# Values times output weights in three 16-bit products, with the step's instructions in a new order, in a decoder layer on one core

## The chip, the cores and the metric

The kernel runs on one core of one Trainium2 chip. The time is device microseconds for one execution, the median of three. Five engines work side by side and meet only at semaphores: TensorE (PE in the profile), VectorE (DVE), ScalarE (ACT), GpSimd (POOL) and SyncE (SP), which issues transfers. Each engine takes its own instructions in program order, so an instruction that waits holds up everything behind it on its engine.

## What is computed

One decoder layer on x of shape 8 x 128 x 256: a gated linear attention with a state per head, a cross attention over 256 positions, and a mixture of experts with a shared expert. Each is added to x after a layer norm. The change touches mostly the first one:

```python
x = x + _L0_attn_ref(_layernorm(x), ...)
x = x + _L0_xattn_ref(_layernorm(x), ctx, mask, mask, ...)
x = x + _L0_ffn_ref(_layernorm(x), ...)

# _L0_attn_ref: 16 heads, 128 key channels, 256 value channels, 128 positions, 8 batches
q = _causal_conv_silu(x @ Wq, qcw, qcb)      # a convolution with 4 taps, then silu
k = _causal_conv_silu(x @ Wk, kcw, kcb)
v = _causal_conv_silu(x @ Wv, vcw, vcb)
q = _l2norm(q); k = _l2norm(k)
alpha = sigmoid(x @ Wa); beta = sigmoid(x @ Wb)
def step(state, inp):
    qt, kt, vt, at, bt = inp
    state = state * at
    err = vt - einsum('bhkv,bhk->bhv', state, kt)
    state = state + bt * einsum('bhk,bhv->bhkv', kt, err)
    ot = einsum('bhkv,bhk->bhv', state, qt)
    return state, ot
out = outs.reshape(b, t, 32 * 128) @ Wo
```

## The kernel before, in words

**The recurrence as matrices.** The scan over 128 positions is not run as a scan. For a head and a batch the kernel forms the 128 x 128 lower part of keys times keys and of keys times queries with its decays (`lm`), inverts the unit triangular matrix by doubling (blocks of 2, 4, ... 128, the "levels"), and so has for each head a 128 x 128 matrix `pt` by which the values are multiplied. The output weights are folded in first: `z` is values times that head's rows of Wo (256 x 256), and the output is `pt` times z.

**Steps and slots.** A step is one head and one group of four batches: 16 heads x 2 groups = 32 steps. Work is software pipelined by hand. In slot k each engine runs a fixed list of calls that belong to up to five steps: `a` is step k+2 (projections, bias, taps of the convolution), `b0` is k+1 (norms, decays, first products), `b` is k (first levels of the inverse, z), `c` is k-1 (last levels, result), `d` is k-2 (output product). Slots -3 to 3 are written out, 4 to 27 run in a hardware loop with four slots in a pass, 28 to 33 are written out again. The order in which an engine's calls stand in `slot(k)` is the order in which they run.

**One slot by engine.** TensorE: `proj_(n)` (L1316), n = 0 to 3 for key, query and the two halves of the values, each six 16-bit products of 512 columns (x and weights split in high and low parts). `z(n)` (L1345), two halves of four 32-bit products of 256 columns. `outp` (L1515), `grams` (L1391) and `grams_later` (L1401) in 32 bits; the levels' products t1 (L1423) and pair (L1430, L1433); `residual` (L1481 to L1483), `y0` (L1493, L1494), `y1` (L1504), `norms` (L1359, L1360), `turn` (L1367), `exponents` (L1376, L1381), `b_first` (L1411). VectorE: twelve taps (L1030), level corrections (L998, L1010, L1013), the two halves of `lm` (`lmul` L1042, `lmul_later` L1053), the two output sums (L1060, L1067), `floor` (L1074) and `terms` (L1084, L1086). ScalarE: four `bias` (L728), the two `zcopy` (L721), the exponentials (L738), `v_silu` (L790), `k_silu` (L768), two squares (L775, L782), copies of t1 (L703 to L714), the logarithm (L754), two table loads. GpSimd: five masked copies `cut` (L501), the 16-bit split of `lm` (`lm_hi` L509 as an addition of zero, `lm_lo` L519), `sq_low_` (L487), four small parts (L527 to L533), and in every other slot the split of the next head's weights (L462, L464, L468).

**PSUM ring.** Banks 0 and 1 (`ubank`) go round z(0) or z(1), zcopy, a projection, its bias and three taps, the next projection, its bias and three taps, and back to z. So `z(0)` waits until the taps of projection 2 are done and `z(1)` until those of projection 3 are.

**Cross attention and experts.** The scores run as 64 units of two heads each. For a unit TensorE makes the scores for the row maximum (`top_scores`, L1638, 32 rows), VectorE reduces them (L1168), TensorE makes the scores again turned (`energies`, L1659, nine units behind), ScalarE takes the exponential (L849), and `values` (L1673, 128 rows by 32 columns) sums. In the experts, for each of 11 tiles of a group: `gate_up` (L1763), `spread_comb` (L1770, 16 rows) and `down` (L1786).

## Time and profile before

| | |
|---|---|
| median of 3 runs | 884.89 us (880.3 to 886.42) |
| the profiled execution | 882.86 us |
| its span | 881.1 us |
| its mean granted clock | 0.979 |
| PE / DVE / ACT / POOL busy | 92% / 80% / 72% / 57% |

The span is the part that the trace covers. The page gives each engine's busy time; other views list the work of a stretch by engine, the chain that ended last, and every instruction with its wait. Back-to-back records of one engine overlap by some 0.05 to 0.1 us, so the distance between two starts is what an instruction costs in a full queue, and its record is longer. A 32-bit product stands in the trace as two records.

### The profile page before, as it was taken

The page shows a single profiled execution, that of the slowest core. Times are in us where ns is not written, and L with a number is a line of the kernel's source. Part 1 is how long each engine was busy: PE and PEld are TensorE (multiplying, and loading weights), DVE is VectorE, ACT ScalarE, POOL GpSimd, SP SyncE. Part 2 cuts the span into 40 slices and gives each one's busy share as a digit, 9 for nine tenths or more (in the row PEclk, how much of TensorE's full clock was granted, in tenths as well). Part 3 has the DMA queues.
Part 4 walks back from the last instruction along what each step waited for, and adds up shares of the span by engine and source line. Part 5 has one row for each costly group of instructions (what it writes and reads, how often), then busy time and mean ns, then how long its engine had stood idle before and what let it go on. Part 6 is the DMA issues. An engine that isn't in the chain of part 4 may idle for free.

```text
span 881.1 us, 21906 instructions
## 1 busy us (share of the span) xinstructions
PE 811.9 (92%) x7458; PEld 526.2 (60%) x7458; DVE 707.2 (80%) x1221; ACT 630.2 (72%) x1052; POOL 501.6 (57%) x633
## 2 busy tenths in 40 slices
PE   3789999999999999999999999999889999989997
PEld 1356766767766777666677667776665333333353
DVE  7588888888888888888888888888566888874747
ACT  3588888888888888888888888888342377765522
POOL 7556959668585775868668596655612223331300
PEclk9799999999999999999999999999999999977999
DMA  5313011010110101001010110000000060000000
GB/s 140 99 27 85 2 38 38 2 37 0 36 35 0 36 0 36 11 25 36 0 36 0 36 36 0 12 2 2 1 2 24 9 108 24 21 21 18 8 24 25
DMA packets 35650, 23.97 MB, mean 27 GB/s; under 512 B 6260, under 2 KB 34644, under 8 KB 35469
## 3 DMA queue, kind: packets, MB, share of 16 engines
q1 hardware_dynamic: 32845, 18.98, 7.7%
q0 software_dynamic: 2752, 4.29, 2.4%
q8 instruction: 32, 0.52, 0.2%
q14 instruction: 21, 0.17, 0.1%
HBM read 22.64 MB, written 1.08 MB: 27 GB/s over the span
## 4 chain that ended last, share of the span: by engine, by line
PE 68%; DVE 14%; issue 9%; ACT 4%; POOL 3%; DMA 1%; SPq 1%; DVEq 1%; ACTq 0%; POOLq 0%
PE psum L1316 13%; PE psum L1345 12%; PE psum L1515 6%; DVE y L1030 6%; PE psum L1673 4%; PE psum L1401 3%; PE psum L1391 3%; DVE ux L1010 3%; PE psum L1423 2%; PE psum L1623 2%; PE psum L1659 2%; PE psum L1430 2%; PE psum L1638 2%; PE psum L1433 2%; PE psum L1763 1%
## 5 line engine op out<-in xcount | busy, mean ns | idle before, releaser
L1030 DVE SCALAR_TENSOR_TENSOR y<-psum,cwh,y 128x508 f32<-128x508 f32 (+2 forms) x384 | 281.6, 740 | 21.6 <-ACT y L728 15.5
L487 POOL TENSOR_TENSOR sql<-sq,sqh 128x1024 f16<-128x1024 f32 x32 | 68.4, 2138 | 135.7 <-ACT sq L775 135.7
L1345 PE MATMUL psum<-wo,vt 128*128 128x256 f32 x512 | 126.0, 389 | 1.2 <-DVE y L1030 1.0
L728 ACT ACTIVATE y<-psum,cwh 128x512 f32<-128x512 f32 x128 | 99.3, 776 | 29.5 <-PE psum L1316 28.7
L501 POOL TENSOR_TENSOR ct<-lm,levels 128x256 f16<-128x256 f32 x160 | 111.0, 711 | 6.8 <-DVE lm L1053 6.8
L1345 PEld LDWEIGHTS psum<-wo,vt 128*128 128x128 f32 x512 | 92.3, 190 | 11.9 <-DVE y L1030 2.0
L1168 DVE TENSOR_REDUCE mx<-psum 128x4 f32<-128x1024 f32 x64 | 77.6, 1220 | 12.7 <-PE psum L1638 12.4
L849 ACT ACTIVATE et<-psum 128x1024 f32<-128x1024 f32 x64 | 65.4, 1023 | 28.9 <-PE psum L1659 27.9
L1010 DVE TENSOR_TENSOR ux<-ux,psum 128x512 f16<-128x512 f16 x64 | 44.0, 687 | 51.9 <-PE psum L1433 50.8
L1316 PE MATMUL psum<-xth,whi 128*128 128x512 f16 x256 | 78.5, 389 | 6.6 <-POOL wlo L468 2.3
L1316 PE MATMUL psum<-xtl,whi 128*128 128x512 f16 x256 | 78.3, 388 | 0.0
L1316 PE MATMUL psum<-xth,wlo 128*128 128x512 f16 x256 | 78.0, 387 | 0.0
L519 POOL TENSOR_TENSOR lml<-lm,lmh 128x1024 f16<-128x1024 f32 x32 | 68.3, 2134 | 0.0
L998 DVE TENSOR_TENSOR ux<-ux,psum 128x512 f16<-128x512 f16 x96 | 65.1, 678 | 1.8 <-PE psum L1433 1.8
L1430 PEld LDWEIGHTS psum<-t1z,ux 128*128 128x128 f16 x768 | 45.6, 98 | 34.0 <-ACT t1z L714 10.0
L509 POOL TENSOR_TENSOR lmh<-lm,zero 128x1024 f16<-128x1024 f32 x32 | 60.5, 1891 | 0.1
L1515 PE MATMUL psum<-zz,pt 128*128 128x256 f32 x256 | 60.5, 379 | 0.0
L1430 PE MATMUL psum<-t1z,ux 128*128 128x64 f16 x768 | 54.0, 193 | 3.9 <-ACT t1z L714 2.0
L1515 PEld LDWEIGHTS psum<-zz,pt 128*128 128x128 f32 x256 | 48.5, 190 | 6.5
L790 ACT ACTIVATE vt<-y 128x1024 f32<-128x1024 f32 x32 | 33.8, 1057 | 23.9 <-issue 16.8
L738 ACT ACTIVATE decay<-psum,rc 128x256 f32<-128x256 f32 x128 | 50.1, 478 | 0.6 <-PE psum L1381 0.5
L1673 PE MATMUL psum<-et,vz 128*32 128x256 f32 x512 | 45.3, 429 | 0.5 <-ACT avs L856 0.3
(220 smaller groups left out, 1957.7 us busy)
## 6 DMA issues: line engine op xcount, KB each, us to landing
wraw<-in_L_attn_Wv SPq DMA_DIRECT2D x32, 128.0 KB, 2.7
wo<-in_L_attn_Wo SPq DMA_DIRECT2D x16, 256.0 KB, 2.8
wraw<-in_L_attn_Wk SPq DMA_DIRECT2D x16, 128.0 KB, 2.5
wraw<-in_L_attn_Wq SPq DMA_DIRECT2D x16, 128.0 KB, 2.9
moved<-avs SPq DMA_DIRECT2D x128, 16.0 KB, 1.8
x<-in_x SPq DMA_DIRECT2D x8, 128.0 KB, 4.0
maskrow<-in_mask_row POOLq DMA_DIRECT2D x1, 1024.0 KB, 5.4
xt<-in_ctx SPq DMA_DIRECT2D x1, 1024.0 KB, 6.4
```

What stands on the lines that cost most here:

```text
L487: g.tensor_tensor(lo, f, hi, ALU.subtract).then_inc(sq_split, 1)
L501: g.tensor_tensor(dst, src, pick.unsqueeze(1).to_broadcast([P, NB, T // (2 * m), m]), ALU.mult).then_inc(masked[l], 1)
L519: g.tensor_tensor(lo, f, hi, ALU.subtract).then_inc(lm_low, 1)
L728: s.activation(y[:, n], ubank[n % 2].rearrange("p (j t) -> p j t", j=NB), ACT.Identity, scale=cwh[:, (a.c // 2) % 2, n, TAPS - 1:TAPS], bi ...
L1010: v.tensor_tensor(changed(r, m), changed(r, m), cx.rearrange("p (a q u) -> p a q u", a=2, u=m), ALU.subtract).then_inc(uxc_sb, 1)
L1030: v.scalar_tensor_tensor(out=y[:, n, :, sh:], in0=u[:, :, 0:T - sh], scalar=cwh[:, (a.c // 2) % 2, n, TAPS - 1 - sh:TAPS - sh], in1=y[:, n ...
L1168: v.tensor_reduce(mx[:, h % 2, g2, 2 * rp:2 * rp + 2].rearrange("p r a -> p (r a)"), pair_of("max", n).rearrange("p r (a s) -> p (r a) s", ...
L1316: mm = t.matmul(ubank[n % 2], w_[:, hr, n, ch, :], x_[:, ch, cols], start=(m == 0), stop=(m == len(ops) - 1))
L1345: mm = t.matmul(ubank[n][:, j * H:(j + 1) * H], vt[:, r, vc, (2 * n + j) * T:(2 * n + j + 1) * T], wo[:, hr, vc, :], start=(vc == 0), stop ...
L1430: mm = t.matmul(half(dst[:, 256 + j * 64:256 + (j + 1) * 64], m), turned(st.c % 2, 0, j), first_half(t1z[:, level - 1, j * T:(j + 1) * T], ...
L1515: mm = t.matmul((ctk, cx)[hf][:, jj * H:(jj + 1) * H], pt[:, j], zz[:, d.c % 2, j], start=True, stop=True)
L1673: mm = t.matmul(avb[ps, gq // 2 * H:(gq // 2 + 1) * H], vz[:, b % 2, st, r, gq], et[:, gn % 4, r, st], start=(gq == 0 and st == 0), stop=( ...
```

## The change

**z in 16 bits.** The values get a high and a low part (`vth`, `vtl`), so do the output weights (`woh`, `wol`), and `z(n)` is now, for each of its four 32-bit products, three 16-bit ones of 256 columns. ScalarE applies silu a second time to write `vth` (`v_high`), and GpSimd subtracts (`v_low_`). GpSimd also scales and splits the output weights of each head, in five pieces that are spread over two slots. The scale of 64 comes out again in `zcopy`.

**Order.** Both halves of `lm` are multiplied at the start of the next slot (`lmul(b, 1)`, `lmul(b, 0)`), the output sums stand side by side, and the third t1 has moved from a slot's end into the next slot, between two other products. On ScalarE the exponentials, biases and squares are exchanged here and there. On GpSimd the four small parts stand after the weights' piece, `lm_hi` is a copy and no longer an addition of zero, and both `lm` parts stand late in the slot.

**Elsewhere.** In cross attention, `energies` stands ahead of `values` from unit 48 on. `spread` and `combt` of the experts are padded from 16 rows to 128 with zeros. The key and value products of cross attention, which fill the last two slots with projections gone, are cut into single calls.

```diff
+        woh = lb("woh", [P, 2, 2, H], F16)
+        wol = lb("wol", [P, 2, 2, H], F16)
+        vth = lb("vth", [P, 2, 2, TOK], F16)
+        vtl = lb("vtl", [P, 2, 2, TOK], F16)
-        spread = fb("spread", [2 * NE, WT, P], F16)
+        spread = fb("spread", [P, WT, P], F16)
...
@@ gpsimd
+            def split_scale(h):
+                pool.wait_ge(w_loaded, h * 64 + 64)
+                (w, wh, wl), o = views(0)
+                g.tensor_tensor(w, w, c64[:].to_broadcast([P, TILES * CH * P]), ALU.mult).then_inc(w_high, 1)
+            def split_scale_out(h):
+                pool.wait_ge(wo_loaded, h * 16 + 16)
+                w, (o, oh, ol) = views(0)
+                g.tensor_tensor(o, o, c64[:].to_broadcast([P, 2 * H]), ALU.mult).then_inc(w_high, 1)
+            def split_high(h, ring, user):
...
+                g.tensor_tensor(cwh[:, ring, :, 0:TAPS], cw[:, h], zero[:].unsqueeze(2).to_broadcast([P, TILES, TAPS]), ALU.add).then_inc(conv_set, 1)
+                g.tensor_copy(wh, w).then_inc(w_high, 1)
+                g.tensor_copy(oh, o).then_inc(w_high, 1)
...
+                def v_low_(b0):
+                    pool.wait_ge(v_act, b0.count(2, 2))
+                    need(pool, z_psum, b0.at(-2).count(2, 2))
+                    f, hi, lo = [q.rearrange("p a n -> p (a n)") for q in (vt[:], vth[:, b0.c % 2], vtl[:, b0.c % 2])]
+                    g.tensor_tensor(lo, f, hi, ALU.subtract).then_inc(v_split, 1)
...
-                    g.tensor_tensor(lmh[:, b.c % 4].rearrange("p j a t -> p (j a t)"), lm[:, b.c % 2].rearrange("p j a t -> p (j a t)"),
-                                    zero[:].to_broadcast([P, NB * 2 * T]), ALU.add).then_inc(lm_high, 1)
+                    g.tensor_copy(lmh[:, b.c % 4].rearrange("p j a t -> p (j a t)"), lm[:, b.c % 2].rearrange("p j a t -> p (j a t)")).then_inc(lm_high, 1)
...
@@ gpsimd, slot
                 cut(b, 1)
+                next_high(f)
+                next_scale(k.at(4))
+                part_high(b0)
+                part_rest(b0)
+                part_middle(b0)
+                part_low(b0)
                 cut(b, 2)
-                parts_()
-                lm_hi()
+                next_low_out(f)
                 cut(b, 3)
-                lm_lo()
+                next_scale_out(k.at(4))
+                v_low_(b0)
                 cut(b, 4)
-                split_next()
-                sq_low_()
+                next_low(f)
+                lm_hi(b)
+                lm_lo(b)
+                sq_low_(a)
                 cut(b0, 0)
...
+            g.memset(combt[:].rearrange("p g n -> p (g n)").bitcast(F32), 0.0).then_inc(late_set, 1)
...
@@ scalar, slot
-                v_silu()
-                ccopy(4)
-                zcopy(0)
-                logs()
-                zcopy(1)
-                ccopy(5)
-                bias(0)
+                v_silu(b0)
+                v_high(b0)
+                ccopy(c, 4)
+                zcopy(b, 0)
+                logs(b0)
+                zcopy(b, 1)
+                ccopy(c, 5)
+                bias(a, 0)
...
@@ vector, slot
-                lmul_later(1)
-                add_out_later(1)
-                level_c(4)
+                add_out(d, 1)
+                lmul(b, 1)
+                lmul(b, 0)
+                level_c(c, 4)
...
@@ tensor
-                            mm = t.matmul(ubank[n][:, j * H:(j + 1) * H], vt[:, r, vc, (2 * n + j) * T:(2 * n + j + 1) * T], wo[:, hr, vc, :], start=(vc == 0), stop=(vc == 1))
+                            ts = slice((2 * n + j) * T, (2 * n + j + 1) * T)
+                            o = ubank[n][:, j * H:(j + 1) * H]
+                            t.matmul(o, vth[:, r, vc, ts], woh[:, hr, vc, :], start=(vc == 0), stop=False)
+                            t.matmul(o, vth[:, r, vc, ts], wol[:, hr, vc, :], start=False, stop=False)
+                            mm = t.matmul(o, vtl[:, r, vc, ts], woh[:, hr, vc, :], start=False, stop=(vc == 1))
...
                 m = n - LAG - 3
+                if n >= 48 and n < UNITS + LAG:
+                    energies(n - LAG)
                 if m >= 0:
                     values(m // 2, m % 2)
-                if LAG <= n < UNITS + LAG:
+                if LAG <= n < 48:
                     energies(n - LAG)
```

TensorE, where one step passes into the next; before, from the second gram (L1401) to the second half of z (L1345), `zz,pt` being the output product:

```order
L1401 MATMUL psum<-kq 128x256 x2
L1515 MATMUL psum<-zz,pt 128x256 x4
L1452 REGISTER_ALU
L1430 MATMUL psum<-t1z,ux 128x64 x4
L1433 MATMUL psum<-ux,t1z 128x64 x4
L1345 MATMUL psum<-wo,vt 128x256 x4
```

After, the same place:

```order
L1486 MATMUL psum<-kq 128x256 x4
L1524 REGISTER_ALU
L1508 MATMUL psum<-ux,ct 128x64 x4
L1593 MATMUL psum<-zz,pt 128x256 x2
L1530 REGISTER_ALU
L1515 MATMUL psum<-t1z,ux 128x64 x4
L1518 MATMUL psum<-ux,t1z 128x64 x4
L1593 MATMUL psum<-zz,pt 128x256 x2
L1431 REGISTER_ALU
L1438 MATMUL psum<-woh,vth 128x256
L1439 MATMUL psum<-wol,vth 128x256
L1440 MATMUL psum<-woh,vtl 128x256
```

Both grams now stand together, the third level's pair stands between the halves of the output product, and z begins its groups of three.

VectorE, from the last projection's taps into the next slot; before (L1042 and L1053 are the halves of `lm`, L1060 and L1067 the output sums, L1010 the fourth level):

```order
L1042 TENSOR_TENSOR lm<-psum,decay 128x512
L1030 SCALAR_TENSOR_TENSOR y<-psum,cwh,y 128x4x127
L1030 SCALAR_TENSOR_TENSOR y<-psum,cwh,y 128x4x126
L1060 TENSOR_TENSOR x1<-x1,psum 128x512
L1030 SCALAR_TENSOR_TENSOR y<-psum,cwh,y 128x4x125
L998 TENSOR_TENSOR ux<-ux,psum 128x2x32x8
L1053 TENSOR_TENSOR lm<-psum,decay 128x512
L1067 TENSOR_TENSOR x1<-x1,psum 128x512
L1010 TENSOR_TENSOR ux<-ux,psum 128x2x16x16
```

After, the same place:

```order
L1129 SCALAR_TENSOR_TENSOR y<-psum,cwh,y 128x4x127
L1129 SCALAR_TENSOR_TENSOR y<-psum,cwh,y 128x4x126
L1129 SCALAR_TENSOR_TENSOR y<-psum,cwh,y 128x4x125
L1097 TENSOR_TENSOR ux<-ux,psum 128x2x32x8
L1148 TENSOR_TENSOR x1<-x1,psum 128x512 x2
L1141 TENSOR_TENSOR lm<-psum,decay 128x512 x2
L1109 TENSOR_TENSOR ux<-ux,psum 128x2x16x16
```

The first half of `lm` and the first output sum have moved behind the last tap, in front of the fourth level.

GpSimd, around the small parts (`parts`, `rest`); before, a slot from the first masked copy `ct` on:

```order
L501 TENSOR_TENSOR ct<-lm,levels 128x128x2
L501 TENSOR_TENSOR ct<-lm,levels 128x64x4
L527 TENSOR_TENSOR parts<-rc,zero 128x8
L529 TENSOR_TENSOR rest<-rc,parts 128x8
L531 TENSOR_TENSOR parts<-rest,zero 128x8
L533 TENSOR_TENSOR parts<-rest,parts 128x8
L509 TENSOR_TENSOR lmh<-lm,zero 128x1024
```

After, in a slot that makes the high parts of the next head's weights:

```order
L544 TENSOR_TENSOR ct<-lm,levels 128x128x2
L479 TENSOR_TENSOR cwh<-cw,zero 128x4x4
L482 COPY cwh<-cb 128x4
L483 CAST whi<-wraw 128x1024
L484 CAST woh<-wo 128x512
L568 TENSOR_TENSOR parts<-rc,zero 128x8
L575 TENSOR_TENSOR rest<-rc,parts 128x8
L582 TENSOR_TENSOR parts<-rest,zero 128x8
L589 TENSOR_TENSOR parts<-rest,parts 128x8
L544 TENSOR_TENSOR ct<-lm,levels 128x64x4
L496 TENSOR_TENSOR wol<-wo,woh 128x512
```

The weights' copies now stand between the first masked copy and the parts. In the other slots the scaling of the weights stands there.

## Rows read from the trace of the kernel before

**Rows 1.** Windows: us of the stretch, busy PE, PEld, DVE, ACT, POOL, clock, DMA.

```profile
80.00:600.00 520.00, 502.87 (x4977) 364.63 (x4976) 451.45 (x779) 433.81 (x750) 366.38 (x400) 1.00 0.07 19
```

**Rows 2.** ScalarE in order of time: start, us, line, operation, wait in brackets.

```profile
294.31 1.06 ACT L790 ACTIVATE vt<-y 128x1024 f32<-128x1024 f32 x1 [0.72 <-issue]
...
310.17 1.06 ACT L782 ACTIVATE sqh<-kq 128x1024 f16<-128x1024 f32 x1
311.12 1.06 ACT L775 ACTIVATE sq<-kq 128x1024 f32<-128x1024 f32 x1
312.90 1.06 ACT L790 ACTIVATE vt<-y 128x1024 f32<-128x1024 f32 x1 [0.72 <-issue]
...
316.81 0.21 ACT L754 ACTIVATE lnn<-n2m 128x8 f32<-128x8 f32 x1 [0.67 <-DVE n2m L1074]
...
320.40 0.28 ACT L759 ACTIVATE rows<-psum 128x128 bf16<-128x128 bf16 x1 [0.78 <-PE psum L1367]
...
331.65 1.06 ACT L790 ACTIVATE vt<-y 128x1024 f32<-128x1024 f32 x1 [0.72 <-issue]
```

**Rows 3.** Chain that ended last, steps at 310: start, us, what.

```profile
307.19 1.29 PE psum L1316 x6
...
311.80 1.81 PE psum L1345 x8
...
313.93 1.81 PE psum L1345 x8
```

**Rows 4.** VectorE in order of time, the same step's end.

```profile
310.05 1.52 DVE L1030 SCALAR_TENSOR_TENSOR y<-psum,cwh,y 128x508 f32<-128x508 f32 x2 [0.25 <-ACT y L728]
...
312.08 0.73 DVE L1030 SCALAR_TENSOR_TENSOR y<-psum,cwh,y 128x500 f32<-128x500 f32 x1
312.73 0.68 DVE L998 TENSOR_TENSOR ux<-ux,psum 128x512 f16<-128x512 f16 x1
313.33 0.68 DVE L1053 TENSOR_TENSOR lm<-psum,decay 128x512 f32<-128x512 f32 x1
...
316.01 0.69 DVE L1010 TENSOR_TENSOR ux<-ux,psum 128x512 f16<-128x512 f16 x1 [1.40 <-PE psum L1433]
...
317.17 0.17 DVE L1084 SCALAR_TENSOR_TENSOR rc<-lnn,gcum 128x8 f32<-128x8 f32 x1 [0.40 <-ACT lnn L754]
```

**Rows 5.** GpSimd in order of time: large operations back to back, and its wait.

```profile
300.02 1.89 POOL L509 TENSOR_TENSOR lmh<-lm,zero 128x1024 f16<-128x1024 f32 x1
...
302.49 2.13 POOL L519 TENSOR_TENSOR lml<-lm,lmh 128x1024 f16<-128x1024 f32 x1
...
312.26 2.15 POOL L487 TENSOR_TENSOR sql<-sq,sqh 128x1024 f16<-128x1024 f32 x1 [7.00 <-ACT sq L775]
```

**Rows 6.** GpSimd: copies, and the first head's weights.

```profile
10.81 0.38 POOL L450 CAST identb<-ident 128x128 bf16<-128x128 f32 x1
...
17.38 2.31 POOL L468 TENSOR_TENSOR wlo<-wraw,whi 128x1024 f16<-128x1024 f32 x1
...
679.53 0.76 POOL L606 COPY vz<-vv 128x64 f32<-128x64 f32 x4
```

**Rows 7.** Chain that ended last, the experts' second group.

```profile
861.26 0.86 PE psum L1763 x4
862.12 0.32 PE psum L1770
862.44 0.54 PE psum L1786 x4
```

**Rows 8.** Chain that ended last, cross attention: full clock, then half.

```profile
761.28 0.57 PE psum L1673 x8
761.84 0.32 PE psum L1659 x4
...
788.10 0.54 PE psum L1659 x4
788.64 1.01 PE psum L1673 x8
```

**Rows 9.** Windows: busy PE, PEld, DVE, ACT, POOL, clock.

```profile
785.00:790.00 5.00, 5.00 (x44) 1.27 (x36) 2.37 (x3) 2.43 (x4) 0.78 (x3) 0.50 0.12 29
```

More of the change, by code:

```diff
@@ L782, in square_high, with v_silu, v_high @@
                     s.activation(sqh[:], kq[:, a.c % 2], ACT.Square, scale=4.0).then_inc(sq_high, 1)
-                def v_silu():
+                def v_silu(b0):
+                    if not b0.valid():
+                        return
+                    act.wait_ge(tapped[2], b0.count(3, 3))
+                    act.wait_ge(tapped[3], b0.count(3, 3))
+                    need(act, v_split, b0.count(1, 0))
+                    s.activation(vt[:], y[:, 2:4].rearrange("p a j t -> p a (j t)"), ACT.Silu).then_inc(v_act, 1)
+                def v_high(b0):
                     if not b0.valid():
@@ new lines, in slot @@
+                level_c(c, 5)
+                tap(a, 0, 1)
+                tap(a, 0, 2)
+                if keys:
+                    kv_stack(b4 + 0, 0)
+                    kv_stack(b4 + 0, 1)
+                level_b(b, 1)
+                tap(a, 0, 3)
+                tap(a, 1, 1)
+                level_c(c, 6)
+                tap(a, 1, 2)
+                tap(a, 1, 3)
+                gate_raw()
+                if keys:
+                    kv_stack(b4 + 1, 0)
+                    kv_stack(b4 + 1, 1)
+                    v_add(b4 + 0)
@@ L1149, in _ @@
+                tap(a, 3, 3)
+                level_b(b, 3)
+                add_out(c, 0)
             slots(dve, slot)
@@ new lines, in k_proj @@
+                    need(pe, k_stack, 2 * (bb - 1))
+                    if m == 1:
+                        need(pe, v_ready, 2 * (bb - 1))
+                    for g2 in range(2):
+                        o = kbank[bb % 2][hh][:, g2 * H:(g2 + 1) * H]
+                        t.matmul(o, wks[:, 2 * hh + g2], ctxs[:, bb], start=True, stop=False)
+                        mm = t.matmul(o, biasr[:, 1, 2 * hh + g2], maskr[:, bb], start=False, stop=True)
+                    mm.then_inc(k_psum, 1)
+                keys = k.i is None and k.c in (STEPS - 1, STEPS)
@@ new lines, in slot @@
+                b4 = (k.c - STEPS + 1) * 4
+                grams(b, 1)
+                b_t1(c, 3)
+                outp(d, 0)
+                b_ux(c, 3)
+                outp(d, 1)
+                z(b, 0)
+                c_t1(c, 4)
+                z(b, 1)
+                c_ux(c, 4)
+                norms(b0)
+                b_first(b)
+                c_t1(c, 5)
+                proj_(a, 0)
+                if keys:
+                    k_proj(b4 + 0, 0)
+                    k_proj(b4 + 0, 1)
@@ new lines, in slot @@
+                c_ux(c, 5)
+                b_t1(b, 1)
+                proj_(a, 1)
+                gate_products()
+                b_ux(b, 1)
+                turn(b0)
+                c_t1(c, 6)
+                exponents(b0, 0)
+                c_ux(c, 6)
+                exponents(b0, 1)
+                if keys:
+                    k_proj(b4 + 1, 0)
+                    k_proj(b4 + 1, 1)
+                    v_proj(b4 + 0)
+                b_t1(b, 2)
+                proj_(a, 2)
+                y0(c)
```

440 lines of the change are left out of this document (200 added, 240 removed).

## The prediction, made before the changed kernel was run

> **What bounds the kernel now.** I read the windows first. From 80 to 600 us, where the 28 regular steps lie, TensorE is busy 502.87 of 520 us, VectorE 451.45, ScalarE 433.81, GpSimd 366.38, at full clock [rows 1]. Then the length of a step: the activation that writes `vt` starts at 294.31 and, two steps on, at 331.65 [rows 2], so a step takes 37.34 / 2 = 18.67 us, and 520 / 18.67 = 27.9 steps lie there. By step: TensorE 18.06, VectorE 16.21, ScalarE 15.58, GpSimd 13.16. TensorE is the bound with 0.61 us of visible idle time, but the others are not far. The chain of waits names what TensorE does when it holds everything up: the two halves of z at 1.81 us each and the projections at 1.29 [rows 3]. VectorE waits 2.46 us a step (18.67 - 16.21). The largest piece is 1.40 us ahead of the fourth level, for TensorE; then 0.40 for the logarithm, 0.25 for a bias [rows 4]. ScalarE waits 3.09, among it 0.72 for the last tap, 0.67 for the norms, 0.78 for the turned rows [rows 2]. GpSimd waits 7.00 us for the squares in a step without weights to split [rows 5], so it has room.
>
> **z in 16 bits, TensorE.** A half of z loses 1.81 us and gains 12 products of 256 columns. Six 16-bit products of 512 columns take 1.29 [rows 3], so one of 256 costs 1.29 / 12 = 0.1075 from below. From above, four bf16 products of 256 columns take 0.54 in the experts, 0.135 each [rows 7]; but they stand behind a product of another row count, and z's new ones stand behind products of their own kind. Twelve cost 1.29 to 1.62 us, so a step gains 2 x 0.52 = 1.04, or 2 x 0.19 = 0.38 at worst. I take 1.04. A gain beyond it is excluded, 256 columns being half of 512. TensorE then needs 18.06 - 1.04 = 17.02 us.
>
> **z in 16 bits, ScalarE.** `v_high` adds one silu of 1024 columns. Two such activations start 0.95 apart (310.17, 311.12) [rows 2]. ScalarE needs 15.58 + 0.95 = 16.53. It stands ahead of the copy for level 4, and behind that copy wait `zcopy(0)`, the table load, the logarithm and the first bias. `zcopy` gets a scale and costs the same.
>
> **z in 16 bits, GpSimd.** Each step adds `v_low_`, like `lml` and `sql` at 2.13 to 2.15, some 2.1 when packed [rows 5]. Each pair of steps adds the output weights, half as wide as the others: scale 0.95 (half of 1.89), copy, difference 1.05. `lm_hi` and the copy of the weights were additions of zero at 1.89 and are now plain copies. The trace has no copy of 1024 columns. From above stands the same 1.89. From below: four copies of 64 columns take 0.76, so at most 0.19 each [rows 6]; a cast of 128 columns took 0.38 at the start of the program [rows 6], but there VectorE was busy in the same memory. Taking off some 0.14 of fixed time gives 0.8 to 1.9 ns a column, so 0.95 to 1.9 us. I take 1.0, by the copies' row, since it lies in undisturbed time. Step cost at 1.0: 13.16 + 2.1 - 0.9 (`lmh`) - 0.45 (half of `whi`) + (0.95 + 0.5 + 1.05) / 2 = 15.2. At 1.9 it is 13.16 + 2.1 + 1.5 = 16.8. Both are below 17.02, so it is place, not amount, that can hurt.
>
> The Trainium skill ("GPSIMD Engine Reference", Performance versus the Vector engine, 3.1) has a one-input body bound by its port at 1.03 cycles an element of 1.2 GHz, but a tight loop at best at 1.8. For 1024 columns an estimate by that page is 0.9 or 1.5 us plus the fixed part; by its second price GpSimd would stand at about 16.2 and not at 15.2. No row here shows which holds.
>
> **The order, VectorE.** It runs the same 28 instructions. What moves: one half of `lm` and one output sum, at 0.60 each (312.73 to 313.33) [rows 4], leave the taps of the last projection and go ahead of the fourth level, where it waited 1.40. The last tap starts at 312.08 and ends at 312.81, the fourth level starts at 316.01, 3.2 us later. In the new order five instructions fill 5 x 0.6 = 3.0 of that. So 1.2 us of wait turn into work, and the work is gone elsewhere; with the bias wait of 0.25 gone too, VectorE's line is 18.67 - 1.45 = 17.2, provided level 4 still starts 3.2 us after the last tap. Its product on TensorE needs ScalarE's copy: last tap, silu 0.95, silu 0.95, copy 0.3, product 0.25 makes 2.5, which fits with 0.7 to spare, unless ScalarE is still in its squares when the last tap ends.
>
> **ScalarE's line.** 16.53 plus what it must still wait. The turned rows' 0.78 stays, since rows still go from VectorE's terms through GpSimd and TensorE; of the 0.67 for the norms between none and all stays. That is 17.3 to 18.0. Between the lines of 17.0, 17.2 and 17.3 to 18.0 I take **17.6 us a step**, a gain of 1.07. For the steps: 27.9, and one more for the z at both ends of the pipeline, where it is partly hidden: 29 x 1.07 = 31.0 us.
>
> **GpSimd's place.** In every other slot 0.3 + copy 1.0 + copy 0.5 now stand between the first masked copy and the small parts, on which TensorE's turn, the exponents and all decays wait; in the slots between, the scaling of 1.89. `lm` is done 3.1 us after the last tap, two masked copies of 0.65 make 4.4, weights 6.3, four parts 7.4 us. Before, TensorE's turn came at 320.1, 7.3 after the tap. So at a price of 1.0 this costs nothing. `lm_hi` and `lm_lo` are not wanted before the next slot.
>
> **Start.** The first projection waits for the first head's low parts, 17.38 + 2.31 = 19.7 us [rows 6]. Ahead of them now stand also the scaling of the output weights (0.95) and their copy (0.5), against 0.9 less for the cheaper copy, and the same stretch is slowed by VectorE: +0.5 to +2, I take **+1.4**.
>
> **Experts and cross attention.** A tile takes 0.86 + 0.32 + 0.54 = 1.72 us [rows 7]. At 0.215 for 512 columns and 0.1075 for 256 it would be 0.86 + 0.215 + 0.43 = 1.5. The 0.22 lie on both sides of the 16-row product; with 128 rows they should go, for the some 9 tiles that TensorE bounds: -2.0. The zeros' memset and the larger load lie beside other work. In cross attention four 32-row products take 0.32 where they run in pairs (2 x 0.107 = 0.21) [rows 8], so 0.1 is lost at a change of shape; `energies` beside `top_scores` saves one change a unit, for some 10 units that are bound by TensorE: -1.0. Together **-3.0**, bounds 0 and -4. The Trainium skill ("TensorEngine Tiling (Array Packing)", Key Properties) says that a change of tiling mode drains the engine; by it all 22 tiles would gain, -4.8, which rows 7 allow only where TensorE is the bound.
>
> One thing can go either way: from 783 to 794 us the granted clock is at half (1.2 GHz), after TensorE had waited for VectorE, and a unit's values take 1.01 instead of 0.57 [rows 8, 9]. If that stretch shortens or another comes, it is up to 5 us. I put it at nothing.
>
> **Sum.** Against the profiled execution, 882.86: -31.0 + 1.4 - 3.0 = 850.3. The median of the three is 2.0 above that execution, so the forecast is **852 us**. A difference of 1% (9 us) is about what can be told from none.
>
> **Rivals.**
> Second silu on the path: ScalarE is not done with the squares when the last tap ends (it had only 0.72 to spare, and now has 0.95 more work in a shorter step). Level 4 then comes later by some 0.6 us. The step is 18.2, the gain 29 x 0.47 = 13.6, the time 884.9 - 13.6 - 1.6 = **870**. It speaks for it that ScalarE would be at 94% of a step of 17.6; against it, that its waits shrink by themselves when it is late. The worst price for the 16-bit products (0.38 a step) gives 872, nearly the same.
>
> Tighter than thought: all four engines pack to VectorE's line and the norms' wait vanishes. Step 17.1, gain 45.5, time **838**.
>
> Slower, by GpSimd: if a copy costs the 1.9 of the addition, the weights take 0.3 + 1.9 + 0.95 ahead of the parts, the turn comes at 4.4 + 3.15 + 1.1 = 8.65 instead of 7.3, and at the slot's end two more long operations push `sql` and the first masked copy some 1.7 beyond the place where norms want them. Every other step then loses 3.0, the mean step is 17.6 + 1.5 = 19.1, the time 884.9 + 29 x 0.43 - 1.6 = **896**. It decides where whi and woh together exceed about 1.6 us (7.3 is met up to there). The 0.38 for a cast of 128 columns speaks for it, the copies of 64 against it.
>
> That the change doesn't do what it says: z's halves shorten, but VectorE's and ScalarE's waits grow by as much and the step stays 18.67: 885 - 1.6 = **883**. Against it speaks the 1.2 us of work put into the 1.40 wait.
>
> **How the numbers follow.** Forecast (843 to 862) 0.50; second silu (862 to 876) 0.20; tighter (below 843) 0.13; unchanged (876 to 893) 0.09; GpSimd (above 893) 0.08. Faster by over 1% is below 876: 0.83; same 0.09; slower 0.08. The range from 836 to 880 leaves out half of the tighter case's lower end (0.05) and 0.15 above; it takes in the clock's 5 us and the price bounds of z.
>
> **What would show it.** A regular step of 17.6 us by the distance of the silus. z's halves at 1.3. VectorE's wait ahead of the fourth level under 0.5. GpSimd's casts of 1024 columns at 1.0, and no wait of TensorE for the turned parts. Tiles of the experts at 1.5. I am wrong if ScalarE shows no wait anywhere and the step is above 18, or if GpSimd is full and TensorE waits for `parts` or `sql`.

## The result, and the profile after

The changed kernel takes **905.92 us** (median of 4 runs, 903.18 to 908.55), the kernel before 885.33 beside it: a ratio of 1.024, with an interval of 1.019 to 1.030. The forecast was 852 us with a range of 836 to 880. The sign was wrong too. The profiled execution took 907.17 us, its span is 905.2, 24.1 more than before.

I read the distances of the `vt` activations first, as the prediction asked. ScalarE of the changed kernel in order of time:

```profile
55.33 1.06 ACT L871 ACTIVATE vt<-y 128x1024 f32<-128x1024 f32 x1 [0.52 <-issue]
79.91 1.06 ACT L871 ACTIVATE vt<-y 128x1024 f32<-128x1024 f32 x1 [0.25 <-issue]
...
291.15 1.05 ACT L871 ACTIVATE vt<-y 128x1024 f32<-128x1024 f32 x1
311.02 1.04 ACT L871 ACTIVATE vt<-y 128x1024 f32<-128x1024 f32 x1
328.75 1.04 ACT L871 ACTIVATE vt<-y 128x1024 f32<-128x1024 f32 x1
347.72 1.04 ACT L871 ACTIVATE vt<-y 128x1024 f32<-128x1024 f32 x1
369.02 1.04 ACT L871 ACTIVATE vt<-y 128x1024 f32<-128x1024 f32 x1
```

Before, every regular step took 18.5 to 19.0 us [rows 2]. Now four steps in a row take 19.87, 17.73, 18.97 and 21.30 us. One of the four is nearly as short as forecast. The other three are not, and this pattern of four repeats, as the loop's body does, which holds four steps. By the same distances the 24.1 us are made up so: +1.65 to the second `vt`; +8.90 in the one step to the third (24.58 in place of 15.68); +12.56 in the 29 steps to the 32nd (555.27 in place of 542.71); +1.0 behind it (270.03 in place of 268.99).

**Once in a pass of the loop.** Waits of the changed kernel, 80 to 600 us, those put down to "issue" (the engine waited for nothing that the profile shows):

```profile
PEld psum L1486 <- issue: 14.4, 5, 3.2
PE psum L1486 <- issue: 12.5, 5, 2.8
```

and one of the five in TensorE's order of time, at the first Gram products (`grams`) of a pass:

```profile
283.86 1.08 PE L1486 MATMUL psum<-kq 128*128 128x256 f32 x4
287.70 1.13 PE L1486 MATMUL psum<-kq 128*128 128x256 f32 x4 [2.76 <-issue]
288.66 0.28 PE L1508 MATMUL psum<-ux,ct 128*128 128x64 f16 x4
288.78 2.01 PE L1593 MATMUL psum<-zz,pt 128*128 128x256 f32 x4
```

Nothing is late there by any semaphore. The loop makes six passes, so five times an engine jumps back. What TensorE's sequencer does just before such a gap stands in the view of the loop's line, L114: the jump itself. First the kernel before, then the changed one (ns min/median/max; the least is the last one, which does not jump):

```profile
L114 PEldq COMPARE_BRANCH  x6: 76/208/243, 196.2 to 570.8; - x6
```

```profile
L114 PEldq COMPARE_BRANCH  x6: 83/3591/3922, 205.2 to 595.1; - x6
```

A jump of 0.2 us has become one of 3.3 to 3.9. The page's section on DMA queues has a row that differs too (packets, MB, share), again before and changed:

```profile
q8 instruction: 32, 0.52, 0.2%
```

```profile
q8 instruction: 78, 1.28, 0.6%
```

So 46 more packets of about 16.4 KB of program were fetched, for 3% more instructions run (22569 against 21906). The granted clock suffers as well: after three of the five gaps (those that end at 209, 288 and 521 us) it goes to its lower level of 1.2 GHz. After the other two the clock stays and TensorE stands once more on "issue", 1.00 and 1.10 us ahead of L1593. Windows of the changed kernel (before, the clock was 1.00 from 80 to 600 us [rows 1]):

```profile
288.00:290.00 2.00, 2.00 (x11) 1.63 (x10) 0.00 (x0) 1.02 (x2) 0.00 (x0) 0.71 0.34 114
290.00:292.00 2.00, 2.00 (x12) 1.48 (x12) 0.74 (x2) 2.00 (x3) 0.62 (x1) 0.50 0.00 0
```

**In steps in which GpSimd scales weights.** VectorE of the changed kernel in order of time, a good step and the next one:

```profile
314.24 0.69 DVE L1109 TENSOR_TENSOR ux<-ux,psum 128x512 f16<-128x512 f16 x1 [0.54 <-PE psum L1518]
...
315.46 0.17 DVE L1165 SCALAR_TENSOR_TENSOR rc<-lnn,gcum 128x8 f32<-128x8 f32 x1 [0.46 <-ACT lnn L835]
...
333.17 1.76 DVE L1165 SCALAR_TENSOR_TENSOR rc<-lnn,gcum 128x8 f32<-128x8 f32 x1 [0.41 <-ACT lnn L835]
334.85 0.15 DVE L1167 SCALAR_TENSOR_TENSOR rc<-lnn,gcol 128x4 f32<-128x4 f32 x1
```

and GpSimd at the second place:

```profile
333.01 1.89 POOL L464 TENSOR_TENSOR wraw<-wraw,c 128x1024 f32<-128x1024 f32 x1
335.08 0.20 POOL L568 TENSOR_TENSOR parts<-rc,zero 128x8 bf16<-128x8 f32 x1 [0.18 <-DVE rc L1167]
```

The instruction that forms `rc` (8 columns) took 0.17 us before [rows 4] and in the step at 315. At 333 it takes 1.76, and ends when GpSimd's scaling ends (334.93 and 334.90). GpSimd's scaling is the `next_scale` that the change put ahead of the parts. So these two engines do not meet at semaphores alone.

Two things could make such a step long: VectorE, held in `rc`, or the small parts, which stand behind the scaling in GpSimd's own list. The chain that ended last runs through VectorE (the 0.90 us of "issue" lie inside the long `rc`):

```profile
333.85 0.90 issue
334.85 0.15 DVE rc L1167
335.00 0.46 DVE ux L1086
```

and TensorE then waits 0.96 us for this `ux` (19 such waits from 80 to 580 us, 15.2 us in all). The parts are as late in the good step, where the casts stand ahead of them: there the last of them ends 7.7 us after the last tap (318.41 and 310.71), in the long step 7.8 us after it (336.27 and 328.48), and yet the steps are 17.73 and 18.97 us. What differs is `rc`.

**In the step to the third `vt`.** GpSimd of the changed kernel:

```profile
65.39 1.89 POOL L464 TENSOR_TENSOR wraw<-wraw,c 128x1024 f32<-128x1024 f32 x1 [6.12 <-DMA wraw<-in_L_attn_Wv]
67.23 0.20 POOL L568 TENSOR_TENSOR parts<-rc,zero 128x8 bf16<-128x8 f32 x1
```

and SP's queue:

```profile
58.66 0.37 SPq L393 DMA_DIRECT2D mask_scratch<-mhl  x1
59.07 0.51 SPq L394 DMA_DIRECT2D bias_scratch<-bhl  x1
59.62 0.52 SPq L379 DMA_DIRECT2D wraw<-in_L_attn_Wk  x1
```

SP issues the third head's weights behind two stores that wait for GpSimd's `flat_rows`, and GpSimd now wants these weights at the head of its list. It waits 6.12 us with the parts and the cuts behind it.

What the forecast said of a single step holds: `z` in rows of 0.11 us a product (311.07, 311.18, ... of L1438 to L1440), GpSimd's casts of 1024 columns at 1.04, VectorE's wait ahead of the fourth level at 0.54 where it was 1.40 [rows 4]. By the windows:

```profile
80.00:600.00 520.00, 467.78 (x5014) 342.30 (x5042) 461.41 (x756) 444.98 (x757) 422.39 (x462) 0.99 0.08 22
```

TensorE is now 52 us idle where it was 17 [rows 1].

### The profile page after: what moved, and what is told of

Same layout as the page of the kernel before. It is cut to its first block, busy times and chain, and to the rows that moved or that the text cites. A ratio compares the mean times of both kernels' runs of the same rounds, so it can differ in the third digit from the quotient of the medians.

```text
span 905.2 us, 22569 instructions
## 1 busy us (share of the span) xinstructions
PE 787.2 (87%) x7677; PEld 515.4 (57%) x7714; DVE 729.6 (81%) x1221; ACT 658.4 (73%) x1084; POOL 572.5 (63%) x714
## 4 chain that ended last, share of the span: by engine, by line
PE 33%; DVE 24%; ACT 21%; issue 15%; POOL 4%; DVEq 1%; SPq 1%; DMA 0%; ACTq 0%; POOLq 0%
DVE y L1129 12%; PE psum L1757 4%; PE psum L1406 4%; ACT L849 4%; ACT L833 3%; ACT kq L849 3%; PE psum L1593 2%; ACT y L809 2%; DVE ux L1097 2%; PE psum L1707 2%; ACT vt L871 2%; PE psum L1743 2%; ACT sqh L863 2%; PE psum L1722 2%; DVE ux L1109 2%
## 5 line engine op out<-in xcount | busy, mean ns | idle before, releaser
L1593 PE MATMUL psum<-zz,pt 128*128 128x256 f32 x256 | 75.1, 418 | 4.9 <-issue 2.1
L1486 PE MATMUL psum<-kq 128*128 128x256 f32 x256 | 64.1, 391 | 12.5 <-issue 12.5
L1438 PE MATMUL psum<-woh,vth 128*128 128x256 f16 x256 | 69.8, 273 | 1.0 <-DVE y L1129 1.0
L1440 PE MATMUL psum<-woh,vtl 128*128 128x256 f16 x256 | 69.8, 273 | 0.0
L1439 PE MATMUL psum<-wol,vth 128*128 128x256 f16 x256 | 69.8, 273 | 0.0
L528 POOL TENSOR_TENSOR vtl<-vt,vth 128x1024 f16<-128x1024 f32 x32 | 68.4, 2136 | 0.0
L784 ACT ACTIVATE t1z<-psum 128x256 f16<-128x256 f32 x96 | 36.9, 384 | 31.3 <-PE psum L1508 30.5
L1486 PEld LDWEIGHTS psum<-kq 128*128 128x128 f32 x256 | 46.2, 191 | 19.5 <-issue 14.4
```

What stands on the lines that cost most here:

```text
L1438: t.matmul(o, vth[:, r, vc, ts], woh[:, hr, vc, :], start=(vc == 0), stop=False)
L1439: t.matmul(o, vth[:, r, vc, ts], wol[:, hr, vc, :], start=False, stop=False)
L1440: mm = t.matmul(o, vtl[:, r, vc, ts], woh[:, hr, vc, :], start=False, stop=(vc == 1))
L1486: mm = t.matmul(ebank[hf][:, jj * 256:(jj + 1) * 256], kq[:, r, j, 0, :], kq[:, r, j].rearrange("p a t -> p (a t)"), start=True, stop=True)
L1593: mm = t.matmul((ctk, cx)[hf][:, jj * H:(jj + 1) * H], pt[:, j], zz[:, d.c % 2, j], start=True, stop=True)
```

## The experiments

There are twelve kernels, e1 to e12. The theory had three parts: **A**, TensorE's loop body has become too long and part of the program is fetched again at each jump back; **P**, `next_scale` stretches VectorE's `rc`; **S**, SP's order makes GpSimd wait in the third head's first step. The rival to A is a wait of the new order that recurs in each pass (**B**), the rival to P that another late term takes its place (**Q**).

### Loop written out, and the scaling moved

```
 def slots(eng, slot):
-    for c in range(-3, 4): ...
-    with eng.Fori(0, LOOPS) as i: ...
-    for c in range(4 + 4 * LOOPS, STEPS + 2): ...
+    for c in range(-3, STEPS + 2):
+        slot(Step(None, c))
```

Expected of the changed kernel with it:

> The changed kernel with its loop over four steps written out, so that no engine jumps back; every instruction and every order as before. Theory A (TensorE, whose loop body has grown, must fetch its program again after each jump back): the gaps of 2.2 to 2.8 us without a releaser ahead of the first Gram products go, with them some 4 to 5 us at each of the six jumps, so about 906 - 26 = 880 us; steps alternate between 17.7 and 19.0 us all through. Rival B (the gap is a wait of the new order that recurs every fourth step, which the trace does not name): the long step every fourth step stays, 906 us.

Expected of the kernel before with it:

> The kernel before with its loop written out in the same way. Theory A: its loop showed no such gap (steps of 18.6 to 18.9 us all through), so nothing to win: 885 us within 4. Rival C (a written-out program is faster or slower whatever the kernel, because code is fetched in another way): it moves by as much as the changed kernel does.

The scaling moved, in the changed kernel:

```
                 next_high(f)
-                next_scale(k.at(4))
                 part_high(b0)
                 ...
                 part_low(b0)
+                next_scale(k.at(4))
                 cut(b, 2)
```

> The changed kernel with GpSimd's scaling of the next head's weights (1.89 us, every second step) placed behind the four small parts of the row sums and not ahead of them. Theory P (the scaling runs beside the DVE instruction that forms rc from two SBUF operands and stretches it from 0.17 to 1.2 to 1.8 us, and in the first step it holds GpSimd in a wait for the weights' DMA): even steps fall from 19.0 to 17.7 us, 14 x 1.25 = 17 us, and the first step gives back 9 us, so 906 - 26 = 880 us. Rival Q (rc only takes the place of something else that is late): the first step alone gives back its 9 us, 897 us.

> Both edits together: loop written out and scaling placed behind the parts. If A and P hold and are independent, 906 - 26 - 26 = 854 us, which is the forecast of 852 us, with steps of 17.7 us all through. If they share a cover, more than 865 us.

| kernel | median us | ratio to before (interval) | steps |
|---|---|---|---|
| e1, changed, written out | 890.67 | 1.006 (1.003 to 1.009) | 18.94, 18.34 |
| e2, before, written out | 879.93 | 0.994 (0.990 to 0.997) | 18.49 |
| e3, changed, scaling late | 894.24 | 1.010 (1.007 to 1.014) | 17.72 to 22.7, five long places |
| e4, both | 871.66 | 0.984 (0.979 to 0.989) | 17.79, 18.33 |
| before, in these runs | 885.07 | | |

Between 80 and 600 us e1 has no wait of TensorE on "issue" over 0.3 us, and no long pass: four steps take 74.56 us where they took 78.35 from 269.37 to 347.72. That is 3.8 us for this jump; over the 29 steps e1 is 17.1 us shorter (538.14 in place of 555.27), 3.4 a jump, and it gained 15.2 by the medians, not 26. So A holds with a smaller price. I had read 4.5 to 5 us a jump against steps of 17.7, and a step of 17.7 stands only once in a pass. Of the kernel before, whose jumps take 0.2 us, writing out took 5.1 us as well (18.71 to 18.49 a step); rival C, that both gain alike, is off by 10 us.

e3 gained 11.7 us and not 26, which is nearer to Q's 897 than to P's 880: 9.4 in the 29 steps and 1.8 in the step to the third `vt`. e4 ended 18 us above its 854. P is shown by the steps and not by e3's time: the even ones fall from 18.94 (e1) to 17.79 (e4). The two causes are not independent. Taken first, the jumps are worth 17.1 us of the 29 steps and the scaling then 14.6 (538.14 to 523.54); taken after the scaling's 9.4, the jumps are worth 22.3 (545.88 to 523.54). But the odd steps stayed at 18.33, and the step to the third `vt` at 22.56. Both misses are in e4's trace. VectorE, then GpSimd, in an odd step:

```profile
334.99 0.20 DVE L1160 SCALAR_TENSOR_TENSOR rc<-lnn,gcum 128x8 f32<-128x8 f32 x1 [0.33 <-ACT lnn L830]
335.12 1.05 DVE L1162 SCALAR_TENSOR_TENSOR rc<-lnn,gcol 128x4 f32<-128x4 f32 x1
```

```profile
335.12 1.04 POOL L478 CAST whi<-wraw 128x1024 f16<-128x1024 f32 x1
```

Both start at 335.12, and the instruction of 4 columns ends with the cast, 1.05 after 1.04. Here too the chain that ended last goes from `rc` to VectorE's `ux` with 0.66 us between them. The Trainium skill ("SBUF — State Buffer", Who interferes with whom) says that a VectorE instruction with two inputs in SBUF contends with a GpSimd instruction that reads SBUF. The traces agree: `rc` reads `lnn` and `gcum` or `gcol`, and takes 0.17, 1.05 or 1.76 us as GpSimd's neighbour lasts. And in the third head's first step:

```profile
60.57 0.20 POOL L584 TENSOR_TENSOR parts<-rest,parts 128x8 bf16<-128x8 f32 x1
65.28 1.89 POOL L459 TENSOR_TENSOR wraw<-wraw,c 128x1024 f32<-128x1024 f32 x1 [4.51 <-DMA wraw<-in_L_attn_Wv]
67.13 1.35 POOL L539 TENSOR_TENSOR ct<-lm,levels 128x256 f16<-128x256 f32 x2
```

The parts are out in time, but the masked copy of level 2 stands behind the same wait, and TensorE waits 4.54 us for it. Moving the scaling had only changed who waits.

### The length of the loop's body, both ways

The kernel before, padded, with eight (e5) or four (e10) further products a step; the changed kernel with one product of `z` left out (e6: the high part of the values times the low part of the weights):

```
                     pe.wait_ge(masked[0], b.count(1, 1))
+                    for j in range(8):          # 4 in e10
+                        t.matmul(bx[:, j:j + 1], ct[:, b.c % 2, 0, j % NB], ident16[:, 0:1], start=True, stop=True)
```

```
                             t.matmul(o, vth[:, r, vc, ts], woh[:, hr, vc, :], start=(vc == 0), stop=False)
-                            t.matmul(o, vth[:, r, vc, ts], wol[:, hr, vc, :], start=False, stop=False)
```

> The kernel before with eight further products of one column each on TensorE ahead of the first level's products (their result is written over): 32 more matrix products in a pass of the loop, as many as the change adds, at a cost of 8 x 0.03 to 0.11 = 0.3 to 0.9 us a step at most. Theory A (the size of TensorE's loop body decides): the instruction queue goes from 32 packets to about 78, TensorE stands idle 2 to 3 us without a releaser once in four steps, and the time rises by 10 to 35 us. Rival B (the new order decides): 32 packets, no such gap, at most 10 us longer.

> The changed kernel without the product of the values' high half with the weights' low half, so that z has two products instead of three (that part of the computation is left out): 32 fewer matrix products in a pass of the loop, TensorE's loop body as long as before, the order of the step as changed. Theory A: 32 packets on the instruction queue, no gap at the jump, 906 - 26 - 32 steps x up to 0.9 = 855 to 880 us. Rival B: the long step every fourth step stays, 880 to 906 us.

> The kernel before with four further products of one column in a step and not eight: half of what the change adds to TensorE's loop body. Theory A says that there is a size from which the jump is no longer free and that the kernel before is below it; it does not say where. Either as before (32 packets on the instruction queue, 885 us) or as with eight (78 packets, 905 us), and nothing between, since a pass either fits or not. Rival (the cost grows with the added instructions): about 895 us, 55 packets.

| kernel | products added to a pass | q8 packets | TensorE on "issue" over 2 us | us |
|---|---|---|---|---|
| before | 0 | 32 | none | 885.33 (median) |
| e10 | 16 | 32 | none | 886.13 (one run) |
| e5 | 32 | 78 | five | 905.28 (one run) |
| changed | 32 | 78 | five | 905.92 (median) |
| e6 | 0 | 32 | none | 888.28 (one run) |

Waits of e5, 80 to 600 us, and its page on the queue:

```profile
PEld psum L1401 <- issue: 18.6, 5, 4.0
PE psum L1401 <- issue: 18.0, 5, 3.8
```

```profile
q8 instruction: 78, 1.28, 0.6%
```

This settles A against B: the old order gets the gaps and the same 78 packets when its body grows by 32 products, and the new order loses them when it shrinks by 32. TensorE's jump takes 3.3 to 3.9 us in e5, 0.2 in e10 and in e6. The step itself was not lengthened by the padding (18.58 and 18.75 us between jumps in e5, as before). e5 pays more for a jump than the changed kernel: its 29 steps take 28.1 us more (570.83 in place of 542.71), with the lower clock after all five gaps; that its time is only 19 to 20 us longer is in part chance, since cross attention's exponents took 4.6 us less in that execution.

e6 stands 8 us above the top of its expectation, 880, since that took 26 us for the jumps: its 29 steps are 17.6 us shorter than the changed kernel's, and the product left out of `z` gives nothing, as its steps are those that P stretches (17.7 to 19.0).

The limit lies between 16 and 32 further products in a pass of the kernel before, and nothing was paid below it. The Trainium skill ("Runtime: NRT & Kernel Launch", Instruction fetch mechanics) has TensorE's instruction memory at 2048 instructions, filled in blocks of 256, and a taken branch out of the window as a fetch that stalls. Packets of 16.4 KB agree with the blocks, and the jumps of 3.3 to 3.9 us with the stall. The size does not give the limit: the trace has 1567 instructions of TensorE in a pass of the kernel before, 1599 in e10's and 1631 in e5's, all fewer than 2048. Whether the length of the body decides or also where it begins, no run separates. The same section calls crossing a block mostly hidden; here written-out code shows no gap, which agrees too.

The traces show the fetch as well. From 200 to 570 us the queue moves no packet in the kernel before, in e10 and in e6, so a body that fits is not fetched again; it moves 43 in the changed kernel and 40 in e5. And in each of the five gaps of both kernels one packet is on its way. The gap of the changed kernel from 284.54 to 287.69:

```profile
q8 instruction: 1, 0.02, 1.7%
```

Packets alone are no sign of a loss: the kernels that are written out fetch 61 to 65 in all, 31 of them from 200 to 570 us in e1, and have no such gap in their steps. By the ten gaps, what costs time is a packet that a jump waits for.

The same steps, with a body of eight steps and three passes:

> The changed kernel with eight steps in the loop's body and three passes in place of four steps and six passes: the same instructions run in the same order, with two jumps back that are followed by another pass and not five. If the price is one for each jump, two long places in the run of 24 steps and 906 - 3 x 3.9 = 894 us; if the price is one for code that is fetched, whichever way it is reached, 906 us, since a body of eight steps is fetched anew in every pass.

902.82 us (ratio 1.019, 1.014 to 1.023) where 894 was expected; 69 packets. Two long places, as many as jumps back that lead into another pass, so the price is one for jumps. But each costs more than the 3.4 us above: the two steps at the first jump take 22.36 and 21.21 us where 37.7 for both is normal, 5.9 us, and at the second 4.7. TensorE's own jump is no dearer (3.4 us both times, in the changed kernel 3.3 to 3.9). The other engines differ. The second instruction queue, q14, carries 58 packets where the changed kernel's has 22, and behind the jumps VectorE (1.9 us, once) and GpSimd (twice, 4.4 us together) stand on "issue" ahead of instructions that have no such wait in the changed kernel:

```profile
POOL ct L544 <- issue: 4.4, 2, 2.3
DVE x L1148 <- issue: 1.9, 1, 1.9
```

So it looks as if the body of eight steps is too long for them as well; no run tests that by itself.

### Both queues and both neighbours put right

e7 is e4 with two more edits, on GpSimd (against the changed kernel):

```
                 cut(b, 1)
-                next_high(f)
-                next_scale(k.at(4))
                 part_high(b0)
                 ...
                 part_low(b0)
                 cut(b, 2)
+                next_scale(k.at(4))
+                next_high(f)
                 next_low_out(f)
```

and on SP, where the block of slot 0 goes behind the loads:

```
-                if k.i is None and k.c == 0:     # waits for rows_split, stores mask_scratch and bias_scratch
-                    ...
                 if k.c % 2 == 0:
                     ...
                         load_w(nxt.head)
                         load_wo(nxt.head)
+                if k.i is None and k.c == 0:
+                    ...
```

> The changed kernel with its loop written out, with GpSimd's scaling and also its two casts for the next head (1.04 and 0.61 us) placed behind the four small parts and the cut of level 2, and with the load of the third head's weights issued by SP ahead of the two stores that wait for GpSimd's split rows. Against e4 (871.7 us): odd steps fall from 18.33 to 17.8 us (14 x 0.53 = 7.4 us), since rc's second instruction no longer ends with the cast of the weights (1.05 us beside 1.04), and the step from the second to the third silu falls from 22.6 to about 18 us, since GpSimd no longer waits 4.5 us for the weights ahead of the cut of level 2. Together 859 to 861 us. Rival: GpSimd, whose odd step has 1.03 us of slack, becomes late itself when it waits for rc before the casts, and the odd step stays above 18.2 us, 867 us.

861.87 us, ratio 0.975 (0.971 to 0.978), just above what was expected. All steps take 17.79 or 17.80 us, the second to third `vt` 16.00. ScalarE of e7 in order of time:

```profile
54.45 1.06 ACT L866 ACTIVATE vt<-y 128x1024 f32<-128x1024 f32 x1 [0.53 <-issue]
70.45 1.06 ACT L866 ACTIVATE vt<-y 128x1024 f32<-128x1024 f32 x1
88.25 1.05 ACT L866 ACTIVATE vt<-y 128x1024 f32<-128x1024 f32 x1
...
301.78 1.05 ACT L866 ACTIVATE vt<-y 128x1024 f32<-128x1024 f32 x1
319.57 1.05 ACT L866 ACTIVATE vt<-y 128x1024 f32<-128x1024 f32 x1
```

VectorE's two forms of `rc` are back at 0.17 and 0.16 on the mean (groups of e7, 80 to 580 us):

```profile
L1160 DVE SCALAR_TENSOR_TENSOR rc<-lnn,gcum 128x8 f32<-128x8 f32 x28 | 4.7, 167 | 9.3 <-ACT lnn L830 9.3
L1162 DVE SCALAR_TENSOR_TENSOR rc<-lnn,gcol 128x4 f32<-128x4 f32 x28 | 4.3, 155 | 0.0
```

The rival, GpSimd late in odd steps, fell: it waits 0.5 us at most for `rc` ahead of the parts, and odd steps are no longer than even ones.

SP's edit alone, in the changed kernel with its loop:

> The changed kernel with one edit on SP alone: the weights' load of the third head ahead of the two stores that wait for GpSimd. In the changed kernel GpSimd stands 6.12 us in the wait for that load and the step is 24.6 us in place of 15.7; with the load issued about 10 us sooner the wait goes and the step falls to 18 to 19 us, 906 - 6 = 900 us. Rival (something else of the first step makes it long, the table load or the clock): 904 to 906 us.

899.38 us (ratio 1.016, 1.011 to 1.021), 6.5 less than the changed kernel's 905.92; the step to the third `vt` is 17.60 us and not 24.58, a little less than expected. S holds.

The price of `z`, on e7, with a fourth product (low half times low half), which makes 16 products a half:

> e7 with a fourth product in z (low half times low half), so that a half of z takes 16 products of 0.11 us, as many passes as the eight 32-bit ones of the kernel before (1.81 us a half). If z stands on the chain that sets the step, as the forecast had it, 2 x 0.43 to 0.52 = 0.9 to 1.04 us a step, 27 to 31 us longer than e7, steps of 18.7 to 18.9 us. Rival: z lies beside other work by now and the new order alone made the step shorter: within 5 us of e7.

887.11 us (ratio 1.001, 0.999 to 1.004), 25.2 longer than e7, with steps of 18.64, 0.85 longer than 17.79: eight products of 0.107. `z` stands on the line that sets the step with its full length. One thing more follows from e8. Its `z` takes nearly as long as the old one, and its step of 18.64 us is no shorter than the 18.49 of the kernel before written out (e2), with TensorE busy for 17.7 us of a step in both. So what e7's step gains over e2's is the 16-bit `z`; the new order, with the work that was added, gains nothing of its own. Whether the old order would have let `z`'s gain through was not tried.

The end of the steps. In the changed kernel the way from the last `vt` to the first exponent is 87.2 us, where it was 84.0. TensorE there:

```profile
660.01 0.28 PE L1508 MATMUL psum<-ux,ct 128*128 128x64 f16 x4 [2.88 <-POOL ct L544]
```

GpSimd is multiplying the context with its mask, eight operations or 5.70 us, ahead of the cuts. e11 is e7 with these eight spread over eight steps:

```
-                if k.i is None and k.c == STEPS - 2:
+                if k.i is None and STEPS - 2 - 2 * B <= k.c < STEPS - 2 and k.c % 2 == 0:
                     pool.wait_ge(ctx_loaded, 16)
-                    for bb in range(B): ctxs[:, bb] *= maskrow[:, bb]
+                    ctxs[:, (k.c - STEPS + 2 + 2 * B) // 2] *= maskrow[:, ...]
```

> e7 with GpSimd's eight products of the context with its mask (5.70 us in one stretch, ahead of the cuts that TensorE waits 2.9 us for in the second last step) spread one by one over eight earlier even steps, where GpSimd has over 2 us of slack. If that stretch is the reason why the way from the last silu to the first exponent is 87 us where it was 84, 2 to 5 us shorter than e7. Rival: the wait is given back behind it, within 1 us of e7.

**853.5 us**, ratio 0.965 (0.961 to 0.969), the fastest kernel of the study, 31.9 below the kernel before. The way to the first exponent is 81.5 us, in e7 88.5. That is 7.0 us, above the 2 to 5 that I expected.

## Why the prediction was wrong

**z's terms were right.** The prediction had a half of `z` go from 1.81 to 1.29 us, 1.04 a step. e8 against e7 gives 0.85 a step for four products a half more, 0.43 a half where the 32-bit ones took 0.52 more. In e7 TensorE is busy 478.25 us of 500 from 80 to 580, 17.02 a step, the forecast's 17.02. ScalarE needs 16.40 (forecast 16.53), GpSimd 15.56 (15.2). The casts' disputed price is 1.04, as chosen between 0.95 and 1.9. The step of 17.6 came out at 17.8 where nothing disturbs it, but in part by luck: 17.6 was picked from ScalarE's line of 17.3 to 18.0, and e8 shows that TensorE's line sets the step, since work added to TensorE alone comes back in full.

**Where the 57 us lie.** The profiled execution was forecast at 850.3 us and took 907.17. Of the 56.9 us, 43.6 lie in the 29 steps (+12.6 where -31.0 was forecast), 9.1 in the start (+10.5 for +1.4) and 4.0 behind the steps (+1.0 for -3.0). Of the 43.6, e1 and e7 give 17.1 to the jumps and 22.0 to `rc`; the rest, 4.4, is the step of 17.8 for 17.6.

**"Both are below 17.02, so it is place, not amount, that can hurt" was right, and the next step failed.** That step, "GpSimd's place ... at a price of 1.0 this costs nothing", added up when GpSimd is done with the parts, 7.4 us after the last tap, and there it was right (7.7 and 7.8). It did not ask what runs beside GpSimd's moved instructions. GpSimd stood idle beside `rc` before (1.04 us, waiting for it); the change put the scaling and the casts there, and `rc` waits, with VectorE's next corrections and TensorE behind it. The evidence was in the prediction's own rows: the cast of 128 columns that "took 0.38 ... VectorE was busy in the same memory" [rows 6] was used as a price for GpSimd and not turned round. It cost 1.15 us in even steps (e1 to e4) and 0.54 in odd ones (e4 to e7), 22 us in all (the 29 steps take 538.14 us in e1 and 516.10 in e7).

**The length of the program has no term in the sum.** The five jumps cost 17.1 us of the 29 steps (e1), or 22.3 when the scaling is out of the way (e3 to e4). Nothing in a view of the kernel before shows how near its loop was to the limit; the number to count was TensorE's instructions, which grow by eight products a step as the trace counts them (24 records of `z` in place of 16).

**"Start", +1.4, looked at the first head's weights only.** The change moves `next_scale` past the parts on GpSimd, and in slot 0 what it waits for is issued by SP behind two stores. +1.65 came by the second `vt`, near the term, and +8.9 right after it.

**Experts and cross attention, -3.0.** From the first to the last gate activation of the experts it is 60.6 us where it was 62.9: -2.3, for the forecast's -2.0, and a tile takes 0.86 + 0.21 + 0.44. So it is in seven of the ten kernels that hold the change; in e1, e7 and e11 it is 62.6 to 63.1, each with a stretch at the lower clock level in the experts (granted clock 0.91 from 820 to 840 us in e1, 0.66 from 801 to 806 in e7, 0.66 from 796 to 801 in e11). The -1.0 of cross attention can't be told: the stretch of exponents took between 104.9 and 114.0 us over the profiled kernels, those with the old order at 104.9, 109.5, 111.7 and 112.3, with stretches at the lower clock level that fall differently each time. Against these stand +3.2 before the first exponent, the cuts behind the context's products.

**Of the rivals** none was it. "Slower, by GpSimd" named the right engine and the right direction, with a mechanism that did not act: it wanted copies at 1.9 us and late parts, and the copies took 1.04 and the parts came in time. "Second silu on the path" is half true: at 311 the chain that ended last runs through `vt` 1.04 and `vth` 0.65, but the step is 17.73 us all the same. Against the written-out kernel before (e2), which is the fair base for what the 16-bit `z` and the order are worth, e7 is 18 us faster.

## What to carry to other kernels

Before a tuned loop grows, count the instructions of its longest engine. Then look at how long its jump back takes and at the instruction queue's packets; if the jump takes microseconds and the loop's passes fetch packets, write the loop out or shorten it before judging the change. When an operation of GpSimd is moved, list what VectorE runs beside it, and suspect first every small VectorE instruction with two SBUF inputs on which others wait. When it is moved forward in its queue, follow what it waits for back through the queue that issues it, in the first steps above all.

## What the runs showed of the hardware that I had not expected

- A loop's body has a sharp limit. 16 further products in a pass cost nothing (886.13 us, 32 packets), 32 cost 19 to 20 us (905.28, 78 packets; one run each). Each jump back of TensorE then takes 3.3 to 3.9 us in place of 0.2, with one packet of program on its way meanwhile, and the lower clock level follows most of these gaps (three of five in the changed kernel, five of five in e5).
- A VectorE instruction of 8 columns and 0.17 us took 1.76 while GpSimd scaled 1024 columns, and one of 4 columns 1.05 beside a cast of 1.04: in both it ended when GpSimd's instruction ended, so the price was what was left of the neighbour's length and not its own.
- Writing out a loop that showed no gap still took 5 us from the kernel before (0.990 to 0.997).
- From a body twice as long a jump cost 4.7 and 5.9 us of the steps against 3.4, while TensorE's own jump stayed at 3.4 us: there VectorE and GpSimd stood on "issue" as well.
